# Gated attention: where the four pieces of the next projection stand in TensorE's order

## The chip, the cores and the metric

One core of one Trainium2 chip runs the whole program. The metric is the device time of one execution in microseconds; lower is better. Three runs of the kernel before gave 629.01, 625.84 and 628.3 us, median 628.3.

## The reference

The input x (2 sequences of 1024 tokens, 256 features) passes four residual blocks: cross attention to a short context, gated attention, an MLP over the context, and a top-1 mixture of 8 experts. The change touches the second alone:

```
dist = softmax(mean(x @ Wr + br, axis=1)); idx = top 4 of 16 heads, per sequence
Q, K, V = (x @ W + b) of the 4 chosen heads, 64 wide each
score = softmax(Q @ K.T / 8) over 1024 keys
O = score @ V;  out = O (4 x 64 features) @ Wo + bo
```

All arithmetic is in float32 precision. The kernel gets it for most products from two fp32r parts: a rounded high part (hi, kh, pTh) and the rest (lo, kl, pTl).

## The kernel before

Gated attention works on 8 items i (2 sequences x 4 chosen heads). For each item it makes scores for 8 tiles of 128 queries against all 1024 keys. One such tile is a unit u = 8 i + q; there are 64. Each engine has its own list of instructions, written out by hand in the order in which it runs them, and semaphores tie the lists.

TensorE (PE), per unit (L1147 on): four matmuls of 512 columns for the scores of u into h_psS (L1155); eight transposes of the normalized probabilities of u-3 into the two halves of h_psT (L1113); eight matmuls for the values of an earlier pair of tiles into h_psO (L1124). Among these stand the pieces of a projection. A projection p makes Q and K of one item for 512 tokens (p = 2 i + chunk) in h_psP, in four pieces: piece 0 and 1 the two contraction halves for the first 256 columns, 2 and 3 for the last 256. Each piece is shown in the trace as two matmuls at L1103. Four units carry the four pieces of one projection, so a projection belongs to units q = 0..3 or q = 4..7; the first of the four carries none. Items are projected ahead: units 8 i to 8 i + 3 make the projection 2 i + 3, the next four 2 i + 4. From unit 52 on there is none left.

The waits that matter: piece 0 waits until the projection before has been read out of h_psP (semaphore qk_lo, L1101). Each half of the transposes waits until VectorE has finished the same half of h_psT of the unit before (pT_lo, L1111). The first half of the values, in odd units, also waits until the output before has been read out of h_psO (o_sb, L1121). The scores of u wait for the exponential of u-2.

ScalarE (ACT), per unit: copies h_psT to h_pTh in two halves (L998), exponential of u (L1025), in even units copies half of the output to h_olo (L1003), in q = 3 and 7 rounds a projection to h_hi (L986), in q = 5 copies the next item's values.

VectorE (DVE), per unit: row maximum of the scores (L1076), reciprocal of the row sum of u-1 (L1069), h_pTl in two halves (L1056), in q = 0 and 4 h_lo of the projection made in the four units before (L1049), in even units from 6 on the output oT (L1064). POOL scales the probabilities. SyncE, when h_lo is there, moves the six parts of a projection to h_qs, h_kh and h_kl by DMA.

Of the kernel before, what the change touches and what calls it, by code (L numbers as in the profile page):

```python
# [877 lines left out]
def gated_attention(nc, top, t, io):  # L878
# [5 lines left out]
    with ExitStack() as ctx:  # L884
# [49 lines left out]
        def upto(eng, s, count):  # L934

            if count > 0:
                eng.wait_ge(s, count)
# [12 lines left out]
        @block.sync  # L950
        def _(sp):
            sp.dma_start(bo[:], io["f_bo"]).then_inc(bo_in, 16)
            sp.dma_start(t["wo"][:], io["f_wo"]).then_inc(t["wo_in"], 16)
            sp.dma_start(t["wr"][:], io["m_wr"]).then_inc(t["c_in"], 16)
            for p in range(2 * NI):
                if p == 1:
                    continue
                upto(sp, s_ps, NQ * (p // 2 - 1))
                sp.wait_ge(qk_lo, p + 1)
                place(sp, p)  # L960
# [134 lines left out]
        @block.tensor  # L1095
        def _(pe):
            def project(p, piece, ps=psP):
                i, ch = divmod(p, 2)
                hf, k = divmod(piece, KD)
                if piece == 0 and ps is psP:  # L1100
                    upto(pe, qk_lo, p)  # L1101
                cols, at = slice(hf * CW // 2, (hf + 1) * CW // 2), i // NA * S + ch * CW
                ins = pe.matmul(ps[:, cols], whead[:, i, k, 0:2 * HD2], xnT[:, k, at + cols.start:at + cols.stop],  # L1103
                                start=(k == 0), stop=(k == KD - 1))
                if piece == 2 * KD - 1:
                    ins.then_inc(qk_ps, 1)

            def transposes(u):
                for hf in range(2):
                    pe.wait_ge(pn_ready, u + 1)  # L1110
                    upto(pe, pT_lo, 2 * u + hf - 1)  # L1111
                    for k in range(HK):
                        ins = pe.transpose(psT[hf][:, k], pr[:, u % 4, (hf * HK + k) * P:(hf * HK + k + 1) * P], ident[:])  # L1113
                    ins.then_inc(pT_ps, 1)

            def values(g, hf):
                i = g // PER
                if hf == 0:
                    pe.wait_ge(pT_lo, 2 * QP * (g + 1))
                    pe.wait_ge(v_ready, i + 1)  # L1120
                    upto(pe, o_sb, g)  # L1121
                for k in range(hf * HK, (hf + 1) * HK):
                    for part in (pTh, pTl):
                        ins = pe.matmul(psO[:, 0:QP * P], vs[i % 2][:, k], part[g % 2][:, k],  # L1124
                                        start=(k == 0 and part is pTh), stop=(k == KT - 1 and part is pTl))
                if hf == 1:
                    ins.then_inc(o_ps, 1)

            for p, ps in ((0, psP), (1, psO)):
                for piece in range(2 * KD):  # L1130
                    project(p, piece, ps)
            def project_v(j):
                b, i = divmod(j, KT)
                upto(pe, v_sb, j - 2)
                if j == 2:
                    pe.wait_ge(qk_lo, 2)
                for k in range(KD):
                    ins = pe.matmul(vbank[j % 3],
                                    xnT[:, k, b * S + i * P:b * S + (i + 1) * P],
                                    whead[:, b * NA:(b + 1) * NA, k, 2 * HD2:3 * HD2],  # L1140
                                    start=(k == 0), stop=(k == KD - 1))
                ins.then_inc(v_ps, 1)

            for j in range(KT):
                project_v(j)

            for u in range(NU):  # L1147
                i, q = divmod(u, NQ)
                if q == 0:
                    for c in range(2):  # L1150
                        pe.wait_ge(qk_in[c], MOVES * (i + 1))
                upto(pe, exp_done, u - 1)
                for hf in range(2):
                    for part in (kh, kl):
                        ins = pe.matmul(psS[u % 2][:, hf * CW:(hf + 1) * CW], qs[i % 2][:, q * P:(q + 1) * P],  # L1155
                                        part[i % 2][:, hf * CW:(hf + 1) * CW], start=(part is kh), stop=(part is kl))
                ins.then_inc(s_ps, 1)
                if u == 0:
                    for piece in range(2 * KD):
                        project(2, piece)  # L1160
                if u < LAG:
                    for j in early[u]:
                        project_v(j)
                if u == LAG:
                    pe.wait_ge(v_sb, 2 * KT)
                ahead = 2 * i + 3 + q // 4
                if ahead >= 2 * NI:
                    ahead = None
                if ahead and q % 4 == 3:
                    project(ahead, 3)  # L1170
                if u >= LAG:
                    transposes(u - LAG)
                if ahead and q % 4 == 2:
                    project(ahead, 1)
                if u >= 5:
                    values((u - 5) // 2, (u - 5) % 2)
                if ahead and q % 4 == 1:
                    project(ahead, 0)
                if ahead and q % 4 == 2:
                    project(ahead, 2)  # L1180

            transposes(NU - 3)
            values(NG - 3, 1)
            transposes(NU - 2)
            values(NG - 2, 0)
            transposes(NU - 1)
            values(NG - 2, 1)
            values(NG - 1, 0)
            values(NG - 1, 1)
# [848 lines left out]
```

## Time and profile before

| | us |
|---|---|
| median of three runs | 628.3 |
| the profiled execution's own time | 627.66 |
| its span, first to last instruction | 625.9 |
| PE busy | 560.3 (90%) |
| DVE busy | 462.0 (74%) |
| ACT busy | 338.2 (54%) |
| POOL busy | 263.4 (42%) |

Gated attention takes the span from about 161 to 393 us. A matmul's row in the trace gives its start and a modelled duration that overlaps the next one; what a matmul costs PE is the distance to the start of the next. "Held by" and "released by" come from semaphore events. Times of the timelines are microseconds from the start of the span.

### The profile page before, as it was taken

How to read it: one execution, taken by the hardware profiler on the slowest of the kernel's cores; microseconds unless marked ns; L12 is line 12 of the kernel's file. 1: busy time of each engine (PE TensorE's matmuls, PEld its weight loads, DVE VectorE, ACT ScalarE, POOL GpSimd, SP SyncE). 2: the span in 40 equal slices, each digit the busy share in tenths (PEclk: the TensorE clock that was granted, in tenths of full speed). 3: DMA queues.
4: the chain of work that ended last, by engine and by line, in shares of the span. 5: the costliest groups of instructions: out<-in, count | busy, mean ns of one | idle time of the engine just before them, and what ended most of it. 6: DMA issues, size and time to landing. Idle time of an engine off the chain costs nothing. (4 is left out here: it accounts for less than half of the span.)

```text
span 625.9 us, 11700 instructions
## 1 busy us (share of the span) xinstructions
PE 560.3 (90%) x3620; PEld 495.7 (79%) x3620; DVE 462.0 (74%) x925; ACT 338.2 (54%) x615; POOL 263.4 (42%) x288
## 2 busy tenths in 40 slices
PE   3779999995899999999999999899747999999993
PEld 3669998984588888888888888666746999999993
DVE  4798999994227888888888898496664775785672
ACT  3345656543247887877877887034303642662351
POOL 4145545670014443444434453114426682683311
PEclk9779999998889999999999999897757999999997
DMA  8245422200422222322223300631416671571110
GB/s 253 52 113 137 125 81 50 51 1 1 114 47 68 51 52 64 83 57 52 51 57 71 76 1 2 233 142 68 136 25 220 210 286 42 207 253 43 34 30 0
DMA packets 25401, 56.99 MB, mean 91 GB/s; under 512 B 5112, under 2 KB 9977, under 8 KB 23304
## 3 DMA queue, kind: packets, MB, share of 16 engines
q1 hardware_dynamic: 21608, 48.80, 26.5%
q0 software_dynamic: 2256, 5.55, 3.0%
q10 hardware_dynamic: 1488, 2.05, 1.1%
q8 instruction: 24, 0.39, 0.3%
q14 instruction: 25, 0.20, 0.1%
HBM read 33.28 MB, written 4.87 MB: 61 GB/s over the span
## 5 line engine op out<-in xcount | busy, mean ns | idle before, releaser
L974 POOL TENSOR_SCALAR h_p<-h_p,h_rs 128x1024 f32<-128x1024 f32 x64 | 72.4, 1131 | 116.1 <-DVE h_rs L1069 116.1
L1076 DVE TENSOR_REDUCE h_nmx<-h_psS 128x1 f32<-128x1024 f32 x64 | 78.1, 1221 | 28.7 <-PE h_psS L1155 27.3
L998 ACT CAST h_pTh<-h_psT 128x512 fp32r<-128x512 f32 x128 | 69.2, 590 | 31.3 <-PE h_psT L1113 31.2
L1056 DVE TENSOR_TENSOR h_pTl<-h_psT,h_pTh 128x512 fp32r<-128x512 f32 x128 | 81.4, 677 | 4.5 <-ACT h_pTh L998 4.5
L1025 ACT ACTIVATE h_p<-h_psS,h_nmx 128x1024 f32<-128x1024 f32 x64 | 72.3, 1129 | 14.0 <-DVE h_nmx L1076 14.0
L1124 PE MATMUL h_psO<-h_pTh,h_vs 128*128 128x256 f32 x256 | 69.9, 306 | 3.0 <-DVE oT L1064 2.2
L1113 PE MATMUL h_psT<-ident,h_p 128*128 128x128 f32 x512 | 67.5, 273 | 1.4 <-DVE h_pTl L1056 1.2
L1113 PEld LDWEIGHTS h_psT<-ident,h_p 128*128 128x128 f32 x512 | 59.3, 141 | 11.4 <-issue 3.3
L1124 PE MATMUL h_psO<-h_pTl,h_vs 128*128 128x256 f32 x256 | 63.6, 282 | 0.0
L371 POOL TENSOR_TENSOR a_p<-a_p,a_rs 128x616 f32<-128x616 f32 x32 | 38.9, 1217 | 57.6 <-DVE a_rs L477 57.6
L1155 PE MATMUL h_psS<-h_kh,h_qs 128*128 128x512 f32 x128 | 55.7, 435 | 0.0
L1124 PEld LDWEIGHTS h_psO<-h_pTh,h_vs 128*128 128x128 f32 x256 | 48.4, 189 | 7.1 <-issue 5.4
L1155 PE MATMUL h_psS<-h_kl,h_qs 128*128 128x512 f32 x128 | 50.7, 396 | 0.0
L1854 PE MATMUL e_psY<-w2h,e_hh 128*128 (+1 forms) x168 | 48.7, 290 | 1.7 <-DVE e_hl L1813 1.7
L1124 PEld LDWEIGHTS h_psO<-h_pTl,h_vs 128*128 128x128 f32 x256 | 48.6, 190 | 0.3
L1762 ACT ACTIVATE e_hh<-e_psT 128x512 fp32r<-128x512 f32 x42 | 22.8, 596 | 47.6 <-PE e_psT L1847 47.6
L1721 POOL DMA_INDIRECT out<-xg,dst x21 | 22.8, 1086 | 60.1 <-DVE xg L1782 59.0
L1854 PE MATMUL e_psY<-w2l,e_hh 128*128 (+1 forms) x168 | 47.0, 280 | 0.0
L1854 PE MATMUL e_psY<-w2h,e_hl 128*128 (+1 forms) x168 | 46.9, 279 | 0.0
L276 ACT ACTIVATE a_p<-a_p 128x616 f32<-128x616 f32 x32 | 23.0, 718 | 37.8 <-DVE a_p L542 37.8
L1902 POOL TENSOR_TENSOR w1l<-wst,w1h 128x1024 fp32r<-128x1024 f32 x16 | 38.8, 2446 | 6.9 <-ACT w1h L1896 6.8
L652 PE MATMUL a_psQ<-a_pT,a_vblk 124*128 124x128 f32 x320 | 39.1, 277 | 1.3 <-DVE a_qlo L462 1.2
(316 smaller groups left out, 1405.2 us busy)
## 6 DMA issues: line engine op xcount, KB each, us to landing
wst<-in_m_w SPq DMA_DIRECT2D x16, 1024.0 KB, 6.3
bias<-in_m_b SPq DMA_DIRECT2D x8, 640.0 KB, 6.8
h_kh<-h_hi SPq DMA_DIRECT2D x30, 128.0 KB, 2.4
h_kl<-h_lo SPq DMA_DIRECT2D x30, 128.0 KB, 2.3
fw<-in_f_w SPq DMA_DIRECT2D x8, 384.0 KB, 3.9
rows<-x_all SPq DMA_DIRECT2D x4, 518.0 KB, 3.5
a_qs<-a_qhi SPq DMA_DIRECT2D x16, 128.0 KB, 2.3
a_qf<-a_qhi SPq DMA_DIRECT2D x16, 128.0 KB, 2.4
```

Of the source, the lines that this page charges most:

```text
L371: pool.tensor_tensor(p3, p3, rs[:, u, :].unsqueeze(2).to_broadcast([P, HH, L]), ALU.mult).then_inc(pn_ready, 1)
L652: ins = pe.matmul(psQ[:, m, b * P:(b + 1) * P], vblk[:, b, m, c, :], pT[:, n % 2, m, c, b * P:(b + 1) * P], start=(c == 0), stop=(c == VC ...
L974: pool.tensor_scalar(pr[:, u % 4], pr[:, u % 4], rs[:, u:u + 1], 0.0, ALU.mult, ALU.add).then_inc(pn_ready, 1)
L998: act.copy(pTh[u // QP % 2][:, hf * HK:(hf + 1) * HK, u % QP * P:(u % QP + 1) * P], psT[hf][:]).then_inc(pT_hi, 1)
L1025: act.activation(pr[:, u % 4], psS[u % 2][:], ACT.Exp, bias=nmx[:, u:u + 1], scale=1.0, accum_out=sm[:, u:u + 1]).then_inc(exp_done, 1)
L1056: vec.tensor_tensor(pTl[u // QP % 2][part], psT[hf][:], pTh[u // QP % 2][part], ALU.subtract).then_inc(pT_lo, 1)
L1076: vec.tensor_reduce(nmx[:, u:u + 1], psS[u % 2][:], AX.X, ALU.max, negate=True).then_inc(max_ready, 1)
L1113: ins = pe.transpose(psT[hf][:, k], pr[:, u % 4, (hf * HK + k) * P:(hf * HK + k + 1) * P], ident[:])
L1124: ins = pe.matmul(psO[:, 0:QP * P], vs[i % 2][:, k], part[g % 2][:, k], start=(k == 0 and part is pTh), stop=(k == KT - 1 and part is pTl))
L1155: ins = pe.matmul(psS[u % 2][:, hf * CW:(hf + 1) * CW], qs[i % 2][:, q * P:(q + 1) * P], part[i % 2][:, hf * CW:(hf + 1) * CW], start=(par ...
L1854: ins = pe.matmul(psY[:, 0:D], h_[:, k], w_[:].rearrange("p a w -> p (a w)")[:, bass.ds(at + k * D, D)], start=(k == 0 and n == 0), stop=( ...
L1902: pool.tensor_tensor(halves(t[f"w1l{e % 3}"][:])[:, :, hf], halves(t["wst"][:, e % 2, 0:KD * FF])[:, :, hf], halves(t[f"w1h{e % 3}"][:])[: ...
```

## The change

In units that carry pieces, all of them now stand between the scores and the transposes: piece 0 in the second unit of four, pieces 1 and 2 in the third, piece 3 in the fourth. Before, piece 0 stood at the end of its unit, piece 1 between transposes and values, piece 2 at the end, and only piece 3 where it is now.

```diff
-                if ahead and q % 4 == 3:
-                    project(ahead, 3)
+                if ahead:
+                    for piece in ((), (0,), (1, 2), (3,))[q % 4]:
+                        project(ahead, piece)
                 if u >= LAG:
                     transposes(u - LAG)
-                if ahead and q % 4 == 2:
-                    project(ahead, 1)
                 if u >= 5:
                     values((u - 5) // 2, (u - 5) % 2)
-                if ahead and q % 4 == 1:
-                    project(ahead, 0)
-                if ahead and q % 4 == 2:
-                    project(ahead, 2)
```

No other engine's list is changed.

## Rows read from the trace of the kernel before

**Rows 1.** The page, parts 1 (busy us, share) and 2 (clock in 40 slices, tenths)

```profile
PE 560.3 (90%) x3620; PEld 495.7 (79%) x3620; DVE 462.0 (74%) x925; ACT 338.2 (54%) x615; POOL 263.4 (42%) x288
...
PEclk9779999998889999999999999897757999999997
```

**Rows 2.** Stretches: length, busy us and count of each engine, clock, DMA

```profile
204.68:348.94 144.26, 142.87 (x970) 128.33 (x969) 126.87 (x210) 114.10 (x215) 64.51 (x62) 1.00 0.26 61
```

**Rows 3.** The waits in 204 to 352 us: total us, times, longest

```profile
PEld h_psO L1124 <- issue: 3.7, 11, 0.4
```

**Rows 4.** Timeline of PE, units 24 to 27: start, us, instruction, count

```profile
257.14 0.39 PE L1155 MATMUL h_psS<-h_kh,h_qs 128*128 128x512 f32 x1
...
259.90 0.40 PE L1155 MATMUL h_psS<-h_kh,h_qs 128*128 128x512 f32 x1
...
260.84 1.04 PE L1113 MATMUL h_psT<-ident,h_p 128*128 128x128 f32 x8
261.94 0.36 PE L1124 MATMUL h_psO<-h_pTh,h_vs 128*128 128x256 f32 x1
...
262.97 0.59 PE L1103 MATMUL h_psP<-xnT,whead 128*128 128x256 f32 x2
263.21 0.58 PE L1155 MATMUL h_psS<-h_kh,h_qs 128*128 128x512 f32 x1
263.63 0.40 PE L1155 MATMUL h_psS<-h_kl,h_qs 128*128 128x512 f32 x1
...
264.34 1.03 PE L1113 MATMUL h_psT<-ident,h_p 128*128 128x128 f32 x8
265.21 0.60 PE L1103 MATMUL h_psP<-xnT,whead 128*128 128x256 f32 x2
...
266.84 0.58 PE L1155 MATMUL h_psS<-h_kh,h_qs 128*128 128x512 f32 x1
...
268.38 1.04 PE L1113 MATMUL h_psT<-ident,h_p 128*128 128x128 f32 x8
...
270.20 0.39 PE L1155 MATMUL h_psS<-h_kh,h_qs 128*128 128x512 f32 x1
```

**Rows 5.** Timeline of DVE, the same units

```profile
258.27 1.23 DVE L1076 TENSOR_REDUCE h_nmx<-h_psS 128x1 f32<-128x1024 f32 x1 [0.41 <-PE h_psS L1155]
...
259.49 1.27 DVE L1056 TENSOR_TENSOR h_pTl<-h_psT,h_pTh 128x512 fp32r<-128x512 f32 x2
260.67 0.74 DVE L1049 SCALAR_TENSOR_TENSOR h_lo<-h_psP,bqk,h_hi 128x512 fp32r<-128x512 f32 x1
261.33 0.47 DVE L1064 SCALAR_TENSOR_TENSOR oT<-h_psO,bv,h_olo 64x256 f32<-64x256 f32 x1
261.72 1.21 DVE L1076 TENSOR_REDUCE h_nmx<-h_psS 128x1 f32<-128x1024 f32 x1
```

**Rows 6.** Timelines of PE and then DVE, unit 17

```profile
235.70 0.36 PE L1124 MATMUL h_psO<-h_pTh,h_vs 128*128 128x256 f32 x1 [0.19 <-DVE oT L1064]
...
234.30 0.74 DVE L1049 SCALAR_TENSOR_TENSOR h_lo<-h_psP,bqk,h_hi 128x512 fp32r<-128x512 f32 x1
235.08 0.48 DVE L1064 SCALAR_TENSOR_TENSOR oT<-h_psO,bv,h_olo 64x256 f32<-64x256 f32 x1
```

**Rows 7.** Timelines of ACT and then DVE, unit 26

```profile
264.97 1.07 ACT L998 CAST h_pTh<-h_psT 128x512 fp32r<-128x512 f32 x2 [0.80 <-PE h_psT L1113]
...
267.18 0.37 ACT L1003 COPY h_olo<-h_psO 64x256 f32<-64x256 f32 x1
...
267.58 0.48 DVE L1064 SCALAR_TENSOR_TENSOR oT<-h_psO,bv,h_olo 64x256 f32<-64x256 f32 x1 [0.56 <-ACT h_olo L1003]
```

**Rows 8.** Timelines of PE and then DVE, unit 5

```profile
195.43 1.23 PE L1113 MATMUL h_psT<-ident,h_p 128*128 128x128 f32 x8 [0.49 <-DVE h_pTl L1056]
...
197.69 0.58 PE L1155 MATMUL h_psS<-h_kh,h_qs 128*128 128x512 f32 x1
...
195.80 0.74 DVE L1049 SCALAR_TENSOR_TENSOR h_lo<-h_psP,bqk,h_hi 128x512 fp32r<-128x512 f32 x1
```

## Prediction

> **What bounds the kernel now.** I read the page first: TensorE (PE) is busy 90% of the span, and its clock is granted nearly in full in the slices of gated attention [rows 1]. The window over units 8 to 51 says more in one line: PE 142.87 us busy of 144.26 at a granted clock of 1.00 (2.4 GHz), VectorE (DVE) 126.87, ScalarE (ACT) 114.10, POOL 64.51 [rows 2]. So inside gated attention the end is set by PE's own list of work, and a change of order there pays only by idle time of PE that it removes, and costs what it adds. No work is added or removed here. The modelled ends hide idle time in the busy sum, so I then went to the waits and to the starts of the matmuls.
>
> The waits show one kind of idle time: the weight load of the values (L1124) stood idle 11 times, 3.7 us in all [rows 3]. There are 11 groups of four units in that window that have projection pieces, so it is once in each group. The timeline of PE gives the place [rows 4]. I call the unit's place in its group q0 to q3 and take group 24 to 27. Scores take 0.94 us (259.90 to the transposes at 260.84), eight transposes 0.87 (264.34 to 265.21). The first score behind a projection is drawn early: it starts at 263.21 and the next only 0.42 later at 263.63, where 0.23 is usual, so the true starts of q2 and q3 are 263.40 and 267.03. The four units are then 2.76, 3.50, 3.63 and 3.17 us long, together 13.06 (257.14 to 270.20). q0 has no piece, so 2.76 is scores, transposes and values (0.95) without idle time. One piece is 0.43 (half of 3.63 - 2.76 in q2). q2 and q3 are thus full; q1 should be 2.76 + 0.43 = 3.19 and is 3.50: 0.31 idle. It stands ahead of the values: they start at 261.94 although the transposes ended at 260.84 + 0.87 = 261.71. What they waited for is o_sb, that is oT, done by DVE at 261.33 + 0.47 = 261.80, after h_lo (260.67 to 261.41) [rows 5]. From the end of a DVE instruction to PE's start is 261.94 - 261.80, about 0.15. In unit 17 oT starts only after h_lo has ended (234.30 + 0.74 = 235.04, oT at 235.08) and the values, whose row names DVE oT as the releaser, follow h_lo's start by 1.40 us where it is 1.27 here (261.94 - 260.67): the idle time is 0.13 longer, 0.44 [rows 6]. These held groups are 5 of the 11, those of even heads. All that could be won: 6 x 0.31 + 5 x 0.44 = 4.1 us.
>
> **The change part by part.** Nothing is issued more or less; DMA, SP and POOL lists are the same, and no piece passes a DMA. Pieces move inside PE's list only.
>
> Piece 3 (q3) stays where it is: 0.
>
> Pieces 1 and 2 (q2) both go ahead of the transposes. PE's sum for q2 stays 3.62. What comes later is the transposes, by 0.43 + 0.43 = 0.86 (from 0.94 to 1.80 after the start of q2; piece 2 passes both the transposes and the values). Behind them, by [rows 4, 7]: ACT's copy of the first half starts 0.63 after the transposes (264.34 to 264.97), h_olo 2.21 after that (267.18, the second copy and exp lie between), oT 0.40 after h_olo (267.18 to 267.58). So oT of q2 starts at 1.80 + 0.63 + 2.21 + 0.40 = 5.04 after the start of q2 and ends at 5.52, against 4.18 to 4.66 before. Two things wait for it. The values of q3 want to start at 3.62 + 0.94 + 0.43 + 0.87 = 5.86, oT and latency allow 5.67: hidden with 0.19 to spare. DVE's maximum of q3 is queued behind oT: it starts 0.39 after oT's start (261.33 to 261.72), at 5.43, where the scores would allow 3.62 + 1.13 = 4.75 (1.13 is 258.27 - 257.14). The two h_pTl follow 1.22 later (258.27 to 259.49) and take 1.27, some 0.65 each, so they end at 7.3 and 7.9. The transposes of the next q0 need these at 6.80 + 0.94 = 7.74 and, second half, 8.18; with latency they are allowed at 7.5 and 8.07. Hidden, but the second by only 0.1. The next maximum would be at 6.80 + 1.13 = 7.93 and DVE is free at 7.85. So DVE has caught up; where oT is of the held kind all is 0.1 later and the cover is just used up. Cost 0, bounds 0 and 0.3 a group.
>
> Piece 0 (q1) is the one that counts. It begins with a wait, L1101: h_lo of the chunk before must have read h_psP (qk_lo). Before the change it came at 262.97, 1.5 us after h_lo's end at 261.41, and did not wait. Now it is reached right after the scores, at 260.84, that is 3.70 after the group's start, while h_lo ends at 4.27 [rows 4, 5]. It can't be sooner: DVE does the maximum of q0 (from 1.13, as soon as the scores allow), reciprocal, two h_pTl and h_lo in this order, and all of it hangs on the scores of q0. Piece 0 starts at 4.27 + 0.15 = 4.42 instead of 3.70: 0.72 idle. Behind it in PE's queue stand the transposes and the values of q1, which had not waited for h_lo. Then piece 0 to 4.85 (0.03 more for the restart of the pipeline, my estimate from the first value matmul after a wait), transposes to 5.75, values to 6.70; oT, allowed at 4.80, is no longer late. q2 starts at 6.70 and before at 263.40 - 257.14 = 6.26: +0.44 a group. In the 5 held groups the group before gives h_lo 0.1 later and the old idle time was 0.13 longer: +0.41. Together 11 x 0.43 = 4.7 us. Bounds: with no latency and no restart 0.26 a group, 2.9 us; with 0.3 more from the side chain of q2, 0.73 a group, 8.0 us.
>
> The Trainium skill has a rule against dropping that wait: PSUM — Partial Sum Buffer, PSUM bank collisions raise a hardware error, says to guard by bank, since a matmul may not write a bank that DVE is reading. h_lo reads all 512 columns of h_psP, one bank. No run here shows what happens without the guard; by the rule the wait is due even where piece 0 touches half of the columns. The page TensorE: Matmul & The Clock Gate, Part 2, also says that weight loads are pulled ahead of matmuls in flight; by that the restart would be free and the sum 0.3 us less. Here the idle time in front of the values is booked on the weight loads themselves [rows 3], so a load does not pass a wait.
>
> The first such group, units 4 to 7, is a case of its own. In unit 5 h_lo ends at 195.80 + 0.74 = 196.54, and PE's transposes had started at 195.43, held by h_pTl [rows 8]. Now they stand behind piece 0: it starts at 196.69, ends at 197.15, transposes to 198.02, values to 198.97. Before, unit 6 started in truth at 197.69 + 0.19 = 197.88: +1.1 us. Units 0 to 3 have the same order in effect (no transposes or values stand between). The last units, 52 on, have no pieces; DVE enters them 0.1 late: +0.1.
>
> Sum: 4.7 + 1.1 + 0.1 = 5.9 us. The stage after begins with loads issued at its start, so the delay is passed on whole. The profiled execution took 627.66 us (span 625.9), 0.6 under the median of 628.3; 5.9 us on the median is 634.2.
>
> **The rivals.** (a) The intended one: piece 0 fills the hole in front of the values and nothing waits. That needs h_lo done by 3.55 after the group's start; gain up to 4.0, 624.3 us. Against it: h_lo starts at 3.53 in this trace and its forerunners are packed without a gap. It decides at h_lo's end: below 3.55 it wins wholly, at 4.0 + 0.15 it is even (0.31 idle either way). 5%. (b) No change that counts: the wait costs only some 0.5 more than nothing, as by the lower bound, and the start-up group is absorbed because ACT and DVE were the ones late there. 1 to 3 us, 629.5 to 631.3. 12%. (c) Slower by much more: moving both pieces in q2 delays oT and the h_pTl of q3 so that the thin covers of 0.19 and 0.1 fail, and that delay comes back in the next h_lo, on which now PE waits. DVE's busy share of 88% [rows 2] speaks for it; that PE's groups become 3% longer speaks against. 0.2 to 0.4 a group on top: 637 to 639. 13%. (d) The clock falls for the added idle time. PE idled 0.49 us ahead of unit 5's transposes [rows 8], and the clock of that slice, the 13th, shows no fall [rows 1]: counted within (c).
>
> **How the numbers follow.** Forecast 70%: 631.5 to 637, likeliest 634.2. With (a) 5%, (b) 12%, (c) 13%. The range of 8 in 10 leaves out (a), half of (b) and the end of (c): 630.5 to 638.0. A measurement of this kernel can tell about 0.5%, 3.1 us: faster by more 5%, within 11%, slower 84%.
>
> **What would show it.** In the changed profile: L1103's first piece in q1 idle before it, released by DVE h_lo, about 0.7 us eleven times and 1.2 once; the idle time of L1124's weight loads gone; period of a group 13.5 in place of 13.06 to 13.18; transposes of q2 at 1.8 after its start and the maximum of q3 no longer waiting for the scores. Wrong if h_lo is released earlier than 4.2 after the group's start, if q3 or q0 gain idle time, or if the stage after takes up the delay.

## The result

The changed kernel took 631.65 us (median of 16 runs, 628.65 to 633.79) against 627.89 us of 16 runs of the kernel before beside them: ratio 1.0059, 95% interval 1.004 to 1.0077, so 3.7 us slower (2.5 to 4.8). A second set of 12 runs gave 1.0038 (1.0018 to 1.0058). The forecast was slower, 634.2 us, by 5.9 us; the range 630.5 to 638.0 holds the time. The sign and the mechanism were right, the size too large by 2.2 us.

The page of the changed kernel, span, PE's share and the clock [rows 1]:

```profile
span 628.6 us, 11699 instructions
...
PE 557.4 (89%) x3619; PEld 492.0 (78%) x3620; DVE 462.2 (74%) x925; ACT 336.7 (54%) x615; POOL 263.0 (42%) x288
...
PEclk9779999998899999999999999997857999999998
```

The stretch from the scores of unit 8 to those of unit 52, as [rows 2] for the kernel before (columns: stretch, length, then busy us of PE, PEld, DVE, ACT, POOL, clock, DMA):

```profile
205.73:354.14 148.41, 143.32 (x970) 127.16 (x969) 126.97 (x210) 112.74 (x214) 64.45 (x61) 1.00 0.26 60
```

It was 144.26 us long and is 148.41, with the same instructions at the same clock. The waits of PE in it, as [rows 3] (us in total, times, longest):

```profile
PEld h_psP L1103 <- DVE h_lo L1049: 9.9, 11, 0.9
...
PE h_psP L1103 <- DVE h_lo L1049: 5.1, 11, 0.5
```

The idle time of the values' weight loads [rows 3] is gone. In its place PE waits for h_lo, 11 times. Timeline of PE, group of units 24 to 27, as [rows 4]:

```profile
259.69 0.40 PE L1155 MATMUL h_psS<-h_kh,h_qs 128*128 128x512 f32 x1
...
262.45 0.40 PE L1155 MATMUL h_psS<-h_kh,h_qs 128*128 128x512 f32 x1
...
264.01 0.70 PE L1103 MATMUL h_psP<-xnT,whead 128*128 128x256 f32 x2 [0.47 <-DVE h_lo L1049]
264.55 1.04 PE L1113 MATMUL h_psT<-ident,h_p 128*128 128x128 f32 x8
265.34 0.36 PE L1124 MATMUL h_psO<-h_pTh,h_vs 128*128 128x256 f32 x1
...
266.37 0.40 PE L1155 MATMUL h_psS<-h_kh,h_qs 128*128 128x512 f32 x1
...
273.18 0.40 PE L1155 MATMUL h_psS<-h_kh,h_qs 128*128 128x512 f32 x1
```

Scores of q1 start at 262.45, piece 0 only at 264.01, with DVE h_lo named as the releaser. The group is 273.18 - 259.69 = 13.49 us long; it was 13.06. Timeline of DVE around it, as [rows 5]:

```profile
257.93 0.47 DVE L1064 SCALAR_TENSOR_TENSOR oT<-h_psO,bv,h_olo 64x256 f32<-64x256 f32 x1 [0.70 <-ACT h_olo L1003]
258.33 1.21 DVE L1076 TENSOR_REDUCE h_nmx<-h_psS 128x1 f32<-128x1024 f32 x1
...
259.53 1.26 DVE L1056 TENSOR_TENSOR h_pTl<-h_psT,h_pTh 128x512 fp32r<-128x512 f32 x2
260.82 1.22 DVE L1076 TENSOR_REDUCE h_nmx<-h_psS 128x1 f32<-128x1024 f32 x1
...
262.03 1.27 DVE L1056 TENSOR_TENSOR h_pTl<-h_psT,h_pTh 128x512 fp32r<-128x512 f32 x2
263.22 0.74 DVE L1049 SCALAR_TENSOR_TENSOR h_lo<-h_psP,bqk,h_hi 128x512 fp32r<-128x512 f32 x1
263.88 0.47 DVE L1064 SCALAR_TENSOR_TENSOR oT<-h_psO,bv,h_olo 64x256 f32<-64x256 f32 x1
```

h_lo starts 3.53 after the group's start (259.69), exactly as before the change (257.14 to 260.67), and ends at 263.96; piece 0 starts 0.05 later. The first row shows what pieces 1 and 2 ahead of the transposes did in the group before: oT waited 0.70 for h_olo, and the maximum, at 258.33, follows it. But the next maximum (260.82) is 1.13 after its scores again, as soon as they allow.

Unit 5, as [rows 8], PE:

```profile
193.74 0.47 PE L1155 MATMUL h_psS<-h_kh,h_qs 128*128 128x512 f32 x1
...
196.56 0.70 PE L1103 MATMUL h_psP<-xnT,whead 128*128 128x256 f32 x2 [1.66 <-DVE h_lo L1049]
197.10 1.04 PE L1113 MATMUL h_psT<-ident,h_p 128*128 128x128 f32 x8
...
198.92 0.40 PE L1155 MATMUL h_psS<-h_kh,h_qs 128*128 128x512 f32 x1
```

It is 5.18 us long (193.74 to 198.92); before it was 197.88 - 193.76 = 4.12: +1.06.

In all, from the first scores to the start of the next stage, gated attention took 224.67 us in place of 219.43, so +5.24. Yet the span grew by 2.7 us only. On PE the next stage starts with four small matmuls (L1575, L1570 after the change, the same code), then come those of L1522 (L1517 after the change). PE before the change, then with it:

```profile
396.28 0.58 PE L1575 MATMUL c_psC<-wr,c_full_ones 128*128 128x8 f32 x4 [1.58 <-POOL c_full_ones L1277]
396.72 2.94 PE L1522 MATMUL c_psR<-wo,oT 128*128 128x256 f32 x8
399.45 2.65 PE L1522 MATMUL c_psC<-wo,oT 128*128 128x256 f32 x8
401.94 1.89 PE L1522 MATMUL c_psR<-wo,oT 128*128 128x256 f32 x8
```

```profile
401.48 0.58 PE L1570 MATMUL c_psC<-wr,c_full_ones 128*128 128x8 f32 x4 [1.58 <-POOL c_full_ones L1272]
401.92 1.97 PE L1517 MATMUL c_psR<-wo,oT 128*128 128x256 f32 x8
403.73 1.89 PE L1517 MATMUL c_psC<-wo,oT 128*128 128x256 f32 x8
405.45 1.89 PE L1517 MATMUL c_psR<-wo,oT 128*128 128x256 f32 x8
```

The sixteen of the first two rows of L1522 took 401.94 - 396.72 = 5.22 us before, and 405.45 - 401.92 = 3.53 after. Before the change a stretch of 3.4 us there was granted 0.5 (1.2 GHz) from 397.6 on; with the change all of it is at 1.0 (2.4 GHz). In both kernels PE had been idle for 1.58 us just before the small matmuls. So 1.69 us came back behind gated attention.

### The profile page after: what moved, and what is told of

Its sections match the earlier page's. It is cut to its first block and busy times, and to the rows that moved or that the text cites. A ratio compares the mean times of both kernels' runs of the same rounds, so it can differ in the third digit from the quotient of the medians.

```text
span 628.6 us, 11699 instructions
## 1 busy us (share of the span) xinstructions
PE 557.4 (89%) x3619; PEld 492.0 (78%) x3620; DVE 462.2 (74%) x925; ACT 336.7 (54%) x615; POOL 263.0 (42%) x288
## 3 DMA queue, kind: packets, MB, share of 16 engines
q10 hardware_dynamic: 1488, 2.05, 1.1%
## 5 line engine op out<-in xcount | busy, mean ns | idle before, releaser
L1124 PE MATMUL h_psO<-h_pTh,h_vs 128*128 128x256 f32 x256 | 68.8, 302 | 1.6 <-DVE oT L1064 1.2
L1124 PE MATMUL h_psO<-h_pTl,h_vs 128*128 128x256 f32 x256 | 63.6, 282 | 0.0
L1155 PE MATMUL h_psS<-h_kh,h_qs 128*128 128x512 f32 x128 | 51.2, 400 | 0.0
L1124 PEld LDWEIGHTS h_psO<-h_pTh,h_vs 128*128 128x128 f32 x256 | 48.4, 189 | 3.1 <-issue 1.7
L1124 PEld LDWEIGHTS h_psO<-h_pTl,h_vs 128*128 128x128 f32 x256 | 48.7, 190 | 0.0
L1103 PE MATMUL h_psP<-xnT,whead 128*128 128x256 f32 x120 | 34.2, 393 | 7.1 <-DVE h_lo L1049 6.7
```

## The experiments

All ratios are to runs of the kernel before on the same chip beside them. "The stretch" is that of units 8 to 52: 144.26 us before the change, 148.41 with it. "Gated attention" is from the first scores to the first instruction of the next stage.

**Is it piece 0 alone?** Two kernels take the change apart. In the first, piece 0 stands where it was:

```diff
-                    for piece in ((), (0,), (1, 2), (3,))[q % 4]:
+                    for piece in ((), (), (1, 2), (3,))[q % 4]:
                         project(ahead, piece)
...
                     values((u - 5) // 2, (u - 5) % 2)
+                if ahead and q % 4 == 1:
+                    project(ahead, 0)
```

> Piece 0 stands at the end of its unit again, pieces 1, 2 and 3 as in the change. Theory (all of the loss is piece 0's wait for h_lo, the later transposes of the third unit are hidden): the stretch from the scores of unit 8 to those of unit 52 is 144.3 us as before the change (it is 148.4 with it), within 0.5 us; unit 5 is 4.1 us long again; the whole is within 0.2% of the kernel before. Rival (pieces 1 and 2 ahead of the transposes delay oT, the next maximum and h_lo): the stretch stays 1 us or more above 144.3 and idle time shows in front of the transposes of the first or the values of the fourth unit of a group.

Its stretch, and the wait that is back (columns as above):

```profile
204.54:348.84 144.30, 142.92 (x971) 128.27 (x970) 125.85 (x210) 113.92 (x215) 64.49 (x61) 1.00 0.26 61
...
PEld h_psO L1124 <- issue: 3.7, 11, 0.4
```

144.30 us, gated attention 219.47: the time of the kernel before to 0.04 us. Ratio 1.0025 (1.0005 to 1.0045), a little above the 0.2% expected, and it comes from no place in gated attention. In this profile the time behind the next stage's start-up is 1.6 us longer than in that of the kernel before; why was not found. Moving pieces 1 and 2 costs nothing in gated attention. The second kernel takes the kernel before and moves piece 0 only:

```diff
                 if ahead and q % 4 == 3:
                     project(ahead, 3)
+                if ahead and q % 4 == 1:
+                    project(ahead, 0)
                 if u >= LAG:
...
                     values((u - 5) // 2, (u - 5) % 2)
-                if ahead and q % 4 == 1:
-                    project(ahead, 0)
```

> Only piece 0 is moved in front of the transposes; pieces 1 and 2 stand as before the change. Theory (piece 0's wait alone): stretch of units 8 to 52 148.4 us, 11 idle times of 0.6 to 0.75 us put down to DVE h_lo, unit 5 5.2 us long, the whole 0.5 to 0.9% slower than the kernel before. Rival (pieces 1 and 2 carry part of the loss): the stretch is 147.4 us or less.

Its stretch is 148.31 us long, and PE again waits 11 times for h_lo:

```profile
PEld h_psP L1103 <- DVE h_lo L1049: 10.0, 11, 0.9
```

Ratio 1.0076 (1.0046 to 1.0105). The rival that shares the loss with pieces 1 and 2 falls in both.

**Is it the place of h_lo in DVE's list?** The change, with h_lo ahead of the two h_pTl:

```diff
+                if q in (4, 0) and u > 0 and 2 * i + 2 + q // 4 < 2 * NI:
+                    project(2 * i + 2 + q // 4)
                 if u >= LAG:
                     low(u - LAG)
                 if u == 1:
                     project(2)
-                if q in (4, 0) and u > 0 and 2 * i + 2 + q // 4 < 2 * NI:
-                    project(2 * i + 2 + q // 4)
```

> The change, and VectorE makes h_lo right after the reciprocal, ahead of the two h_pTl of that unit, in place of behind them. h_lo then ends about 3.1 us after the group's start in place of 4.27. Theory (TensorE waits for h_lo's place in VectorE's list): piece 0 starts at 3.70 with no wait, the second half of the transposes at 4.57 just after its h_pTl (4.27 + 0.15 = 4.42), no idle time is left in the group: stretch of units 8 to 52 144.26 - 4.1 = 140.2 us, unit 5 about 4.3 us, in gated attention 4 us less than before the change, 9 less than with it. Rival (VectorE is nearly full, the delay only changes its place: the h_pTl come 0.65 later and the transposes wait for them in place of piece 0 for h_lo): the stretch is 144 us or more, idle time of PE put down to DVE h_pTl.

```profile
205.75:346.19 140.44, 140.44 (x971) 128.07 (x969) 125.37 (x210) 113.78 (x215) 64.38 (x61) 1.00 0.27 63
```

The busy sum alone does not show that no idle time is left, since modelled ends can cover some. The starts do: the four units of a group need 2.76 + 3.19 + 3.63 + 3.17 = 12.75 us by the rows of the kernel before, and the eleven groups here are 12.75 to 12.79 us long. Timelines around unit 13, PE and then DVE (start, us):

```profile
221.25 0.40 PE L1155 MATMUL h_psS<-h_kh,h_qs 128*128 128x512 f32 x1
...
222.19 0.59 PE L1103 MATMUL h_psP<-xnT,whead 128*128 128x256 f32 x2
222.62 1.04 PE L1113 MATMUL h_psT<-ident,h_p 128*128 128x128 f32 x8
223.41 0.36 PE L1124 MATMUL h_psO<-h_pTh,h_vs 128*128 128x256 f32 x1
...
224.45 0.40 PE L1155 MATMUL h_psS<-h_kh,h_qs 128*128 128x512 f32 x1
...
220.84 0.73 DVE L1049 SCALAR_TENSOR_TENSOR h_lo<-h_psP,bqk,h_hi 128x512 fp32r<-128x512 f32 x1
221.49 1.28 DVE L1056 TENSOR_TENSOR h_pTl<-h_psT,h_pTh 128x512 fp32r<-128x512 f32 x2
```

Piece 0 follows the scores at once (221.25 + 0.94 = 222.19), the second half of the transposes (222.62 + 0.44) comes after the end of h_pTl (222.77). Ratio 0.9929 (0.9902 to 0.9956): 4.4 us faster than the kernel before, with the lowest median of this study (622.23 us).

**Or a place of piece 0 where h_lo is done?** DVE as it was, piece 0 between transposes and values:

```diff
-                    for piece in ((), (0,), (1, 2), (3,))[q % 4]:
+                    for piece in ((), (), (1, 2), (3,))[q % 4]:
                         project(ahead, piece)
                 if u >= LAG:
                     transposes(u - LAG)
+                if ahead and q % 4 == 1:
+                    project(ahead, 0)
                 if u >= 5:
```

> Pieces 1, 2 and 3 as in the change, piece 0 between the transposes and the values of its unit; VectorE as it was. Piece 0 is then reached at 4.57 after the group's start, later than h_lo's end plus latency (4.42), and the values at 5.00, later than oT (4.80 to 4.95). Theory: no idle time in any group, stretch of units 8 to 52 140.2 us, unit 5 about 4.3 us, gated attention 4 us shorter than before the change. Rival (the hole in front of the values isn't set by oT's end, so work in front of it only pushes it on): the stretch is 144 us again.

```profile
205.09:345.40 140.31, 140.31 (x970) 127.66 (x969) 125.36 (x210) 113.91 (x214) 64.52 (x61) 1.00 0.27 63
```

140.31 us, groups of 12.74 to 12.78 us, so again no idle time; ratio 0.9947 (0.9925 to 0.9969). That its whole gain is the smaller (the intervals overlap), with the same stretch to 0.13 us, fits what the next stage does in the two, shown below. The hole of the kernel before could be filled, with this very piece; the change put it 0.87 us too early in the list.

**Do the two repairs add?** Both edits together.

> Both of the two repairs at once: VectorE makes h_lo ahead of the two h_pTl, and piece 0 stands between transposes and values. Theory of the places: the transposes come at 3.70 after the group's start again, and now the h_pTl that they need are 0.65 later (first half ends at 3.67, second at 4.27, plus 0.05 to 0.15), so the second half, due at 4.14, waits 0.2 to 0.3 us in each of 11 groups: stretch of units 8 to 52 142.5 to 143.5 us, worse than either repair alone (140.4 and 140.3). Rival (each repair removes its own wait and they add or at least don't hurt): 140.4 us or less.

They do not: the stretch is 143.78 us. In the timeline of PE the second unit of a group is 3.5 us long (unit 13, 220.86 to 224.37) where 3.19 is its work, and the weight loads of its transposes are idle:

```profile
PEld h_psT L1113 <- POOL h_p L974: 4.3, 12, 0.4
...
PEld h_psT L1113 <- issue: 2.1, 12, 0.2
```

So each group waits 0.3 us, now for h_pTl (the row names POOL, which had long been done). 143.78 is 0.3 above the range expected; ratio 0.9988 (0.9957 to 1.0019). Each of the two repairs is right only where the other is left out.

**Does h_lo first help the old order?** Old order on PE, h_lo first on DVE.

> TensorE's order as before the change, VectorE makes h_lo ahead of the two h_pTl in the first and fifth unit of a head. Theory (the hole of the old order is set by oT, and oT keeps its place behind all three): stretch of units 8 to 52 144.3 us as before, ratio 1.000, so that the gain of h_lo first needs the moved piece. Rival (h_lo first is a gain by itself, it lets oT or the h_pTl go earlier): stretch 142.5 us or less.

```profile
204.72:349.02 144.30, 144.30 (x971) 127.16 (x969) 126.86 (x210) 115.09 (x215) 64.38 (x62) 1.00 0.26 61
...
PEld h_psT L1113 <- POOL h_p L974: 4.1, 11, 0.4
...
PEld h_psT L1113 <- issue: 2.0, 11, 0.2
```

The number came out (144.30, ratio 1.0019, 1.0001 to 1.0036), the reason did not. I had expected the hole to stay in front of the values. It went to the transposes: their weight loads are idle 11 times twice (the first row names POOL, which had long been done; the second half waits for h_pTl), and no row is left for L1124. Note that the window gives PE as busy for all of its 144.30 us although each of the 11 groups holds 0.3 us of idle time. oT has not moved: in unit 13 it ends 1.90 us after the unit's scores start (220.53 to 222.43), and the values start 2.05 us after them (222.58); in the kernel before these were 1.90 and 2.04 (259.90 to 261.80 and 261.94). So oT still allows the values no earlier start, and the new wait stands ahead of them in time that PE would have lost to oT. That the new wait costs no more than the old one, to 0.01 us, is a coincidence of this kernel's durations.

**How much does a later h_lo cost?** The change, with oT ahead of h_lo (the two calls in DVE's loop swapped).

> The change, and VectorE makes oT ahead of h_lo in the first and fifth unit of a head, so that h_lo is about 1.05 us later (it must then wait for ScalarE's h_olo, at 4.15 after the group's start: oT 4.19 to 4.66, h_lo to 5.33). Theory (each microsecond of h_lo's end is a microsecond of TensorE): 11 groups by 1.05 us, stretch of units 8 to 52 148.4 + 11.5 = 159.9 us, idle time in front of piece 0 put down to DVE h_lo 26 us in place of 15 on both rows together, about 2.6% slower than the kernel before. Rival (TensorE has slack that takes part of it): stretch under 157 us.

```profile
204.25:365.22 160.97, 143.33 (x971) 127.15 (x969) 127.53 (x210) 112.72 (x215) 64.38 (x61) 1.00 0.24 55
...
PEld h_psP L1103 <- DVE h_lo L1049: 22.4, 11, 2.2
PE h_psP L1103 <- DVE h_lo L1049: 17.6, 11, 1.7
```

160.97 us, 12.56 more than with the change: 1.14 a group where 1.05 was expected, nothing absorbed. Six groups grew by 1.04, as expected, and the five of even heads by 1.26. Both rows together are 40.0 us idle where I had expected 26: weight load and matmul count the same time, so the delay stands in both rows (for the change they are 9.9 and 5.1, and each grew by 12.5). Ratio 1.0266 (1.0233 to 1.03).

**What gives time back behind gated attention?** The kernel before, delayed at the end of gated attention by matmuls whose results nobody uses, 14 of them:

```diff
             values(NG - 1, 1)
+            pe.wait_ge(qk_lo, 2 * NI)
+            for _ in range(14):
+                pe.matmul(psP[:, 0:CW // 2], whead[:, NI - 1, 0, 0:2 * HD2], xnT[:, 0, 0:CW // 2], start=True, stop=True)
```

> The kernel before with 14 more projection matmuls of 256 columns (0.43 us each) behind the last values of gated attention, whose results nobody uses: a delay of the next stage by about 5.2 us, as the change gives, without any change inside. Theory (the stages behind give 1.5 to 2.5 us back, because the half-clock stretch that hits the first matmuls of the next stage at 397.6 us is missed when they come 5 us later): ratio 1.0055 to 1.0065, first 8 matmuls of the next stage 2.0 us in place of 2.9 us, span 628.5 us. Rival (a delay is passed on whole, and what the two profiles show is chance): ratio 1.0083, on average over the timed runs.

Its next stage, PE:

```profile
403.28 0.58 PE L1578 MATMUL c_psC<-wr,c_full_ones 128*128 128x8 f32 x4 [0.65 <-POOL c_full_ones L1280]
403.72 1.97 PE L1525 MATMUL c_psR<-wo,oT 128*128 128x256 f32 x8
405.53 1.89 PE L1525 MATMUL c_psC<-wo,oT 128*128 128x256 f32 x8
```

Gated attention with the pad is 224.63 us long (+5.20, as with the change), and the first eight matmuls take 1.8 us to the next row, not 2.7. Ratio 1.006 (1.0032 to 1.0087), the value expected of the theory, though the interval reaches the rival's 1.0083. The span of this one execution was 631.3, not 628.5. One thing besides the time differs: with the pad PE is idle for 0.65 us before the stage, not 1.58, so the pad alone does not tell a later start from a shorter pause. With 8 matmuls in place of 14:

> The same with 8 such matmuls, a delay of about 2.6 us. Theory of the give-back by place in time: the first matmuls come at 399.3, inside the stretch that was at half clock before (397.6 to 401.0), so either less or nothing is given back: ratio 1.0015 to 1.004. Rival (passed on whole): 1.0041.

Gated attention +2.53 us, the stage starts at 399.24, again at full clock and after 0.65 us of idle time; ratio 1.0027 (1.0005 to 1.0049), which holds both the value with all of the 1.68 us given back (1.0014) and that with none (1.0041). The profile goes against the picture behind both expectations: the matmuls came inside 397.6 to 401.0, and in this profile all of the 1.68 us came back, where less or nothing was expected. So the half-clock stretch does not stand at a fixed time of the program, waiting for matmuls to run into it. The kernel before against itself, and the change once more:

> The kernel before, unchanged, as a second program beside itself. Any theory: ratio 1.000. In its profile: if the half-clock stretches of TensorE in the stages after gated attention stand at the same places of the span as in the first profile (397.6, 428.3 and 445.4 us), they are tied to the program's time; if they stand elsewhere by several us, they fall by chance and what they cost differs from execution to execution.

> The change again, unchanged. If the later stages give time back because of when they start: no half-clock stretch at the first matmuls of the next stage (there is one at 397 us in both profiles of the kernel before, none in that of the change), ratio under 1.0083 once more, about 1.006. If that was chance: the stretch can stand there, and the ratio tends to 1.0083.

The first: ratio 0.9997 (0.9979 to 1.0015), half-clock stretches at 397.4, 428.1 and 445.1 us, 0.2 to 0.3 from the first profile. The second: stretch 148.42 us, no half clock at the first matmuls, ratio 1.0038 (1.0018 to 1.0058).

Over the 13 profiles, from the start of the next stage to its first normalized rows (xg):

| stage starts at, us | kernels | PE idle before the four small matmuls, us | to xg, us |
|---|---|---|---|
| 392.35 | piece 0 between transposes and values | 1.59 | 10.31 |
| 393.12 | the change, h_lo first | 1.59 | 8.63 |
| 395.65 to 395.95 | before twice, piece 0 back, h_lo first with the old order, both repairs | 1.58 | 10.31 |
| 399.24 | pad of 8 | 0.65 | 8.63 |
| 401.09 to 401.86 | the change twice, piece 0 only | 1.58 to 1.59 | 8.62 to 8.63 |
| 402.89 | pad of 14 | 0.65 | 8.63 |
| 412.79 | oT ahead of h_lo | 1.59 | 8.62 |

It is one of two values, 1.68 us apart, and kernels that start the stage at the same time have the same value. The first two rows of the table, two kernels that start the stage 0.77 us apart (first row, then second):

```profile
392.74 0.58 PE L1572 MATMUL c_psC<-wr,c_full_ones 128*128 128x8 f32 x4 [1.59 <-POOL c_full_ones L1274]
393.18 2.52 PE L1519 MATMUL c_psR<-wo,oT 128*128 128x256 f32 x8
...
393.51 0.58 PE L1570 MATMUL c_psC<-wr,c_full_ones 128*128 128x8 f32 x4 [1.59 <-POOL c_full_ones L1272]
393.95 1.97 PE L1517 MATMUL c_psR<-wo,oT 128*128 128x256 f32 x8
```

The pause is the same here and the value is not, so the length of the pause is not what decides between these two. The pads keep PE's old order in gated attention and have the full clock too. So the give-back goes with when the stage starts, not with the change as such; this is a reading over 13 profiles, no kernel moved the start alone with all else kept. What rule puts the half-clock stretch there was not found: 392.35 has it and 393.12 has not. Later on, a long half-clock stretch (from 445.4 in the kernel before) differs between two profiles of one and the same kernel (in the change from 452.1 for 27.3 us, in its second profile from 449.4 for 34.1), and single spans of the change were 628.6 and 631.7. From xg to the end the 13 profiles take 217.9 to 221.7 us. That part was not explained; timed runs average it.

## Why the prediction was right, and where its sum was off

- PE as the bound, a single hole a group in front of the values, set by oT: right. Each of the two repairs removes 3.8 to 4.0 us from the stretch, near the 4.1 forecast as the most that could be won.
- Piece 0 meets h_lo, and transposes and values stand behind it: right. h_lo ended 4.27 after the group's start as forecast. Latency (0.15 taken) and restart (0.03) were 0.05 and 0.11, so q2 starts 6.68 after the group (259.69 to 266.37), 6.70 forecast: two errors that cancel, which is luck. A group without the longer old hole grew by 0.43.
- The held groups: forecast +0.41, measured +0.31. The failed step is "the group before gives h_lo 0.1 later". The maximum of q0 was ready in time in those groups too (DVE at 233.84, 1.13 after the scores at 232.71), so h_lo was not later and only the old, longer hole was lost. 11 groups: 148.41 - 144.26 = 4.15 in place of 4.7.
- Pieces 1 and 2 at no cost, by a thin cover: right, shown by the first experiment (144.30).
- Units 4 to 7: +1.1 forecast, +1.06. The last units +0.1 forecast, 0 measured.
- Gated attention: 4.15 + 1.06 = 5.2, measured 5.24, in place of 5.9.
- "The stage after begins with loads issued at its start, so the delay is passed on whole": this step failed. It looked at the loads, not at PE's clock. The stage's first matmuls had been at half clock before and no longer were, 1.68 us. 5.24 - 1.68 = 3.56 us, or 1.0057; measured 1.0059 and, in the second set, 1.0038 (1.0018 to 1.0058). Without the 1.68 it would be 1.0083, outside both intervals. Whether the stretch stands there in every timed run is not shown; the profiles are single executions. The same sum gives 1.0266 for oT ahead of h_lo (18.4 - 1.7 = 16.7 us), measured 1.0266, and 1.0056 for the pad of 14, measured 1.006; for the kernel that moves piece 0 only it gives 1.0055, measured 1.0076, still inside the interval. Of all kernels it falls outside the interval for one, that with piece 0 back (1.0001, measured 1.0025). The prediction had named this as a sign of being wrong, "if the stage after takes up the delay". The forecast was 2.2 us too large; by the profiles this step makes 1.7 of it and gated attention 0.7, together 2.4.
- Rivals: (a) fell, though its idea is sound with piece 0 elsewhere. Its point of no gain or loss is mis-stated too: 0.31 idle means a start of piece 0 at 3.70 + 0.31 = 4.01, so h_lo's end at 3.86 with the latency taken, not 4.0 + 0.15. (c) fell, no idle time appeared in q3 or q0 beyond 0.03. (d) fell, the clock of the stretch is 1.00 as before. (b) was the nearest in size, for a reason it did not name.

## What to carry to other kernels

A piece of work fills a hole only if its own inputs are ready by then: write down, from one period of the trace, when each wait is released, and put the piece between its own release and the next one's. Here 0.87 us later in the list turned a loss of 4.2 us into a gain of 4.0 in the stretch. The two engines' lists were tied so closely here that a repair in either list worked alone and both together undid each other, so each order is to be worked out against the other list as it will be. A busy sum equal to the stretch does not show that idle time is gone; the distances between starts do. And a delay of some microseconds need not be passed on as it is when a later stage begins with matmuls after a pause: look there at the granted clock in both profiles before the sum is believed.

## What was not expected of the hardware

The clock granted to the first matmuls of the next stage went with the time at which the stage began: 5.22 us or 3.54 us for the same 16 matmuls after the same pause of 1.58 or 1.59 us (393.18 to 398.40 and 393.95 to 397.49 in two kernels that begin the stage 0.77 us apart), and the same value, to 0.01 us, for the five profiles that begin it within 0.3 us of one another (395.65 to 395.95). PE went on 0.05 us after h_lo's end with a projection piece; with the values it had been about 0.15 after oT's end.
